# GNN kernel on one Trainium2 core: relational edges sorted by type, multiplied tile by tile, and gathered back in destination order

## The reference, cut to what matters

```python
x = _layernorm(x + sage3(x))          # per layer: mean of x[src] over dst, @ Wl + bl + x @ Wr
x = _layernorm(x + gin(x))            # gelu(x[src] + edge_attr @ bond_W) * edge_weight1, summed, MLP
x = _layernorm(x + gcn2(x))           # x[src] weighted and summed, layer norm, time embedding
x = _layernorm(x + rgcn2(x))

def _rel_conv(h, W, loop_w, b, src, dst, etype, relu):     # W: (8, 128, 128)
    h_rel = jnp.einsum('ni,rio->rno', h, W)
    msg = h_rel[etype, src]
    agg = jax.ops.segment_sum(msg, dst, num_segments=h.shape[0])
    out = agg + h @ loop_w + b
    return jax.nn.relu(out) if relu else out
```

## Time and profile before

| | us |
|---|---|
| three runs | 6101.26, 6092.66, 6088.61 |
| median | 6092.66 |
| profiled execution | 6085.37 |
| its span | 6083.6 |
| setup and round 0 (SAGE) | 0 to 624 |
| round 1, round 2 (SAGE) | 624 to 1120, 1120 to 1793 |
| round 3 (GIN) | 1793 to 2726 |
| rounds 4, 5 (GCN) | 2726 to 3439, 3439 to 4307 |
| rounds 6, 7 (RGCN) | 4307 to 5166, 5166 to 6084 |

### The profile page before, as it was taken

The page is one execution under the profiler, slowest core; times in us unless marked ns, Lnnn a source line. Parts: engine busy times, 40 slices in busy tenths (PEclk is TensorE's granted clock), DMA queues, the critical chain, the costliest instruction groups (busy, mean ns, idle before and its releaser), DMA issues.

```text
span 6083.6 us, 129573 instructions
## 1 busy us (share of the span) xinstructions
PE 4641.5 (76%) x25128; PEld 2978.4 (49%) x25129; DVE 3341.9 (55%) x10510; ACT 2416.6 (40%) x4967; POOL 1918.2 (32%) x1886
## 2 busy tenths in 40 slices
PE   5889678566668888866667477887688897788885
PEld 3555345233335555534444244554466674666662
DVE  4334233355644545545777477776454554676775
ACT  1333233144426777634555256564211111222233
POOL 5550663444213333006440233410323320423310
PEclk9999799788979999988889788898799999999998
DMA  3554466354424444324444255553333333333332
GB/s 101 171 173 143 143 206 217 99 159 158 148 82 128 144 142 137 127 93 127 143 143 132 76 178 189 185 182 123 109 108 120 113 112 125 96 111 113 104 106 97
DMA packets 443920, 815.61 MB, mean 134 GB/s; under 512 B 70873, under 2 KB 76819, under 8 KB 443829
## 3 DMA queue, kind: packets, MB, share of 16 engines
q1 hardware_dynamic: 389172, 697.28, 34.4%
q0 software_dynamic: 54656, 117.32, 7.7%
HBM read 480.10 MB, written 334.22 MB: 134 GB/s over the span
## 4 chain that ended last, share of the span: by engine, by line
PE 42%; issue 18%; DVE 15%; DVEq 8%; another core or an unknown queue 6%; ACT 4%; DMA 2%; POOL 2%; ACTq 2%; SPq 1%; POOLq 0%
PE p_agg L1115 7%; PE p_edge L1102 6%; PE p_agg L1117 6%; PE p_tr L1102 5%; PE p_agg L1148 4%; DVE onehot L1549 3%; DVE stats L1636 3%; PE p_wide L1235 2%; DVEq L371 2%; PE p_agg L1141 2%; PE p_dense L1191 2%; DVEq L1549 2%; PE p_wide L1179 2%; DVE u L1675 1%
## 5 line engine op out<-in xcount | busy, mean ns | idle before, releaser
L1115 PE MATMUL p_agg<-onehot,msg 128*128 128x512 f16 (+1 forms) x2848 | 1187.9, 417 | 793.4 <-DVE onehot L1549 490.6
L1549 DVE TENSOR_SCALAR onehot<-iota,dst_f,negbase 128x512 f16<-128x512 f16 (+1 forms) x2848 | 1040.3, 419 | 981.8 <-issue 382.7
L679 POOL DMA_INDIRECT raw<-node_s,src_i x980 | 960.8, 980 | 1843.1 <-DMA node_s<-o 695.6
L1117 PE MATMUL p_agg<-onehot,msg 128*128 128x512 f16 (+1 forms) x2848 | 1191.7, 418 | 25.8 <-issue 25.0
L1115 PEld LDWEIGHTS p_agg<-onehot,msg 128*128 x2848 | 290.2, 102 | 1171.1 <-issue 1035.3
L679 POOL DMA_INDIRECT raw<-node_x,src_i x392 | 378.6, 966 | 637.9 <-DMA feature<-more_masked 303.5
L1148 PE MATMUL p_agg<-h_in,w 128*128 128x512 f32 x784 | 470.6, 685 | 88.9 <-issue 46.1
L880 ACT ACTIVATE o<-v_ring,nmr,rstd 128x128 f32 (+1 forms) x1176 | 472.3, 482 | 59.0 <-DVE nmr L1652 47.3
L1636 DVE BATCH_NORM_STATS2 stats<-v_ring 128x6 f32 (+1 forms) x1960 | 418.2, 279 | 55.0 <-DVE v_ring L1626 19.0
L1117 PEld LDWEIGHTS p_agg<-onehot,msg 128*128 x2848 | 290.4, 102 | 280.6 <-issue 113.1
L1514 DVE SCALAR_TENSOR_TENSOR hid<-type_in,p_wide 128x512 f32<-128x512 f32 (+2 forms) x456 | 260.1, 617 | 289.8 <-PE p_edge L1102 190.6
(11 more groups left out here) (260 smaller groups left out, 7806.3 us busy)
## 6 DMA issues: line engine op xcount, KB each, us to landing
node_s<-o SPq DMA_DIRECT2D x392, 256.0 KB
h_in<-feature SPq DMA_DIRECT2D x392, 256.0 KB
feature<-u SPq DMA_DIRECT2D x294, 256.0 KB
node_x<-o SPq DMA_DIRECT2D x294, 256.0 KB
res_in<-node_x SPq DMA_DIRECT2D x294, 256.0 KB
h_in<-node_s SPq DMA_DIRECT2D x196, 256.0 KB
h_t<-dinv_scratch SPq DMA_DIRECT2D x196, 256.0 KB
h_in<-in_x SPq DMA_DIRECT2D x98, 256.0 KB
```

The source lines that it names most:

```text
L679: nc.gpsimd.indirect_dma_start(out=raw[:, (e % RING) * BATCH + j, :], out_offset=None, in_=src_d, in_offset=bass.IndirectOffsetOnAxis(ap=s ...
L1115: nc.tensor.matmul(p_agg[:, a, :], tile_ap(msg, t, 0, D), oh, start=first, stop=True, skip_group_check=True)
L1117: return nc.tensor.matmul(p_agg[:, a, :], tile_ap(msg, t, D, 2 * D), oh, start=False, stop=True, skip_group_check=True)
L1549: return V.tensor_scalar(tile_ap(onehot, slot), iota[:, :], dst_f[:, bass.ds(t, 1)], negbase[:, bass.ds(it * 2 + a, 1)], ALU.subtract, ALU ...
```

## The change

Between rounds 1 and 2 the edges of each batch are sorted by type on the chip. DVE and PE count, for each edge, the edges of its batch with a lower type or with the same type ahead of it; that gives its place in the sorted batch (`place_i`), the type of each place (`type_rows`, to DRAM), and for each batch a list of 14 *slots* in two words: which of the seven sorted tiles slot n works on. The type of slot n is n minus its tile, since sorted tiles hold types in steps. In round 2 POOL scatters the source numbers to their sorted places (196 scatters of 128 numbers), and they are read back as `sorted_i`.

In the relational rounds POOL gathers the rows in sorted order and copies them to `edge_fixed`. PE turns all seven tiles at once; DVE makes 14 masks of 128 columns instead of 16 of 512 or 384; PE makes 14 products instead of 56. Tile and type of a slot come from registers. ACT and DVE write the two fp16 parts to `stage`, ACT stores it to DRAM (`edge_dram`, 458 KB a batch), and POOL gathers the rows back into `msg` in destination order, seven more indirect DMAs a batch (`bring_back`). Batches run one ahead of before (`later_batches`). PE waits, before the items of each half, until the last batch that the half needs is back. In the text of the diff, `before` in names stands for earlier edges.

```diff
+SLOTS = BATCH + REL - 1
...
+            def scatter_sources(e):
+
+                if e == 0:
+                    pool.wait_ge(places_ready, 1)
+                for t in range(e * BATCH, (e + 1) * BATCH):
+                    nc.gpsimd.indirect_dma_start(
+                        out=sorted_dram, out_offset=bass.IndirectOffsetOnAxis(ap=place_i[:, t:t + 1], axis=0),
+                        in_=src_i[:, t:t + 1], in_offset=None).then_inc(scattered, 16)
+
+            def typed_edges(r, src_d):
+                q = S[r]
+
+                def gather(e):
+                    if e >= RING:
+                        wait(pool, q.batch_in, e - RING + 1)
+                    gather_batch(r, src_d, e, sorted_i)
+                    if e >= RING:
+                        wait(pool, q.masked_done, SLOTS * (e - RING + 1))
+                    pool.dma_start(type_in[:, e % RING, :], type_dram[e:e + 1, :].partition_broadcast(P)
+                                   ).then_inc(gathered[e % RING], 16)
+
+                def hand_over(e):
+                    slot = e % RING
+                    pool.wait_ge(gathered[slot], 16 * (per_batch[r] * (e // RING + 1) + landed_before[r]))
+                    if e:
+                        wait(pool, q.et_done, e)
+                    nc.gpsimd.tensor_copy(edge_fixed, raw[:, slot * BATCH:(slot + 1) * BATCH, :]
+                                          ).then_inc(q.batch_in.semaphore, 1)
+
+                def bring_back(e):
+                    wait(pool, q.staged, 16 * (e + 2))
+                    wait(pool, q.backed, 16 * BATCH * e)
+                    for t in range(e * BATCH, (e + 1) * BATCH):
+                        nc.gpsimd.indirect_dma_start(
+                            out=msg[:, t, :], out_offset=None, in_=edge_dram[0:(e + 1) * BATCH * P, :],
+                            in_offset=bass.IndirectOffsetOnAxis(ap=place_i[:, t:t + 1], axis=0),
+                        ).then_inc(q.backed.semaphore, 16)
+
+                pool.wait_ge(sorted_in, 16)
+                for e in range(2):
+                    gather(e)
+                    hand_over(e)
+                bring_back(0)
+                gather(2)
+                hand_over(2)
+                for e in range(1, BATCHES):
+                    if e + 2 < BATCHES:
+                        gather(e + 2)
+                    bring_back(e)
+                    if e + 2 < BATCHES:
+                        hand_over(e + 2)
...
                 for e in range(BATCHES):
...
                     gather_batch(r, src_d, e)
...
+                    if r == 2 and e >= RING:
+                        scatter_sources(e - RING)
...
                     if rel:
-                        for part, (j0, j1) in enumerate(QUARTERS):
-                            wait_apart(act, q.masked_used, e * (2 * REL) + (REL * (part + 2)))
-                            nc.scalar.activation(
-                                msg[:, bass.ds(e * BATCH + j0, j1 - j0), 0:D],
-                                related[part][:, 0:(j1 - j0) * D].rearrange("p (j d) -> p j d", d=D), ACT.Copy
-                                ).then_inc(q.hi_done.semaphore, 1)
+                        mine = bass.ds((e % 2) * BATCH, BATCH)
+                        wait_apart(act, q.masked_used, e + 2)
+                        nc.scalar.activation(stage[:, mine, 0:D],
+                                             related[:, 0:BATCH * D].rearrange("p (j d) -> p j d", d=D), ACT.Copy
+                                             ).then_inc(q.hi_done.semaphore, 1)
+                        wait_apart(act, q.lo_done, e + 1)
+                        wait_apart(act, q.staged, e * 16 + 16)
+                        nc.scalar.dma_start(
+                            edge_dram[bass.ds(e * (BATCH * P), BATCH * P), :].rearrange("(p j) d -> p j d", j=BATCH),
+                            stage[:, mine, :]).then_inc(q.staged.semaphore, 16)
...
-                def products(e, part):
-                    j0, j1 = QUARTERS[part]
-                    for m in range(REL):
-                        wait(pe, q.masked_done, e * (2 * REL) + (part * REL + m + 1))
-                        for j in range(j1 - j0):
-                            last = nc.tensor.matmul(
-                                related[part][:, j * D:(j + 1) * D], masked[m][:, j * P:(j + 1) * P],
-                                w[:, m, :], start=m == 0 and j == 0, stop=True, skip_group_check=True)
-                        last.then_inc(q.masked_used.semaphore, 1)
+                def products(e):
+
+                    these = slot_list(pe, PT, e)
+                    wait_apart(pe, q.lo_done, e)
+                    nc.tensor.matmul(related[:, 2 * HALF - 1:2 * HALF], ident[:, :], ident[:, 0:1], start=True, stop=True,
+                                     skip_group_check=True)
+                    for n in range(SLOTS):
+                        tile = slot_tile(pe, these, n)
+                        wait_apart(pe, q.masked_done, e * SLOTS + (n + 1))
+                        last = nc.tensor.matmul(
+                            related[:, bass.ds(tile * D, D)], masked[n],
+                            tile_ap(w, (n - tile).with_bounds(min_val=0, max_val=REL - 1)),
+                            start=n == 0, stop=True, skip_group_check=True)
+                    last.then_inc(q.masked_used.semaphore, 1)
...
                     t0, i0, i1 = these[:3]
+                    if rel:
+                        last_batch = pe.snap(((((t0 + (i1 - i0) * GROUP + (EVERY - 1)).with_bounds(
+                            min_val=0, max_val=TILES - 1) * ROW7) >> 16) & 31).with_bounds(
+                            min_val=0, max_val=BATCHES - 1))
+                        wait_apart(pe, q.backed, last_batch * (16 * BATCH) + 16 * BATCH)
...
-                        if rel:
-                            wait_apart(pe, q.lo_done, these[0] * 2)
...
-                def masks(e, part):
-                    j0, j1 = QUARTERS[part]
-                    wait_apart(dve, q.et_done, e * 2 + (part + 3))
-                    cols = slice(0, (j1 - j0) * P)
-                    for m in range(REL):
-                        wait(dve, q.masked_used, e * (2 * REL) + (part * REL + m + 1))
+                def masks(e):
+                    these = slot_list(dve, PT, e)
+                    wait_apart(dve, q.et_done, e + 1)
+                    wait_apart(dve, q.masked_used, e + 1)
+                    for n in range(SLOTS):
+                        tile = slot_tile(dve, these, n)
                         V.scalar_tensor_tensor(
-                            out=masked[m][:, cols],
-                            in0=flat(type_in[:, bass.ds(e % RING, 1), j0 * P:j1 * P]), scalar=float(m),
-                            in1=p_wide[:, part, cols], op0=ALU.is_equal, op1=ALU.mult
+                            out=masked[n],
+                            in0=types_flat[:, bass.ds((e % RING) * (BATCH * P) + tile * P, P)],
+                            scalar=colf[:, bass.ds((n - tile).with_bounds(min_val=0, max_val=REL - 1), 1)],
+                            in1=turned_batch[:, bass.ds(tile * P, P)], op0=ALU.is_equal, op1=ALU.mult
                             ).then_inc(q.masked_done.semaphore, 1)
...
                 if rd.kind == SAGE:
                     sage_round(r, rd.layer, False)
+                    if rd.layer == 1:
+                        sort_types()
```

297 lines of the change are left out of this document (210 added, 87 removed).

## The result

The changed kernel takes 7109.34 us (median of 4 runs, 7095.45 to 7134.94) against 6090.64 (median of 4, 6080.6 to 6101.26: the three of before and one more): a ratio of 1.1682, 95% interval 1.165 to 1.1713. Slower, as forecast, but by 1019 us where the forecast had 254, and beyond the range's upper end of 6640.

The account below looks back on a forecast made before the run. PE was taken to bound the first relational round, with DVE close behind in the second. Seven terms summed to +254 us on 6085.4, with 7.3 for the median 6346 us; range 5985 to 6640.

Parts of the forecast that it names:

- Term 3: First relational round: 14 register-addressed products instead of 56 shorten each batch's burst by 2.5 us, −70 us (−224 to +40).
- Term 7: Relational rounds: seven more indirect DMAs per batch fit POOL but slow the other engines, +129 us (0 to 314).
- term 2: Round 2: issuing 196 scatters of source numbers costs other engines 1.7 us per run of seven, +41 us (0 to 67).
- term 4: Second relational round: masks no longer made a batch ahead, so products come 2.0 us later per batch, +57 us (−116 to +90).
- Term 1: Between rounds 1 and 2: sorting in DVE's program ahead of round 2 costs +22 us (0 to 40).
- Terms 5 and 6: Computed tile numbers before each half's items, +50 us (0 to 67), and a lower granted PE clock, +25 us (0 to 50).
- term 5: PE before each half's items: the wait for returned rows is never late, but computing tile numbers costs +50 us (0 to 67).
- B: Rival: products were the bound and slots cost only the datapath's 0.28 us, 5835 us; chance 0.23 with half-way cases.
- C: Rival: slots are register-bound, but POOL's DMA issues cost the other engines nothing, 6176 us; chance 0.16.
- D: Rival: POOL's chain of staging, gathering back and hand-over becomes the bound, 6600 us (6480 to 6700); chance 0.14.

## Why the prediction was wrong

The sign was right, and so was the suspicion that POOL's issues cost others; the size was wrong by a factor of four. Term 3, the gain that the change was made for, had the wrong sign, so the right sign of the sum came from costs alone. PE's *turn* below is the time of PE from the end of a pair's row work, over products and transposes, to the next one-hot matmul, a mean over the batches of a round: before 14.7 and 14.2 us, without bring-back 16.9 and 22.4, changed 20.9 and 26.3, fixed slots without bring-back 8.3 and 13.5 (these kernels ran on different chips; 2% of a turn is 0.3 to 0.5 us).

**Term 7, and with it term 2, are where it failed.** "The other engines pay again what term 2 shows" took a run of seven as the unit of price. The rows it stood on the earlier trace rows were right, but a run of fourteen isn't two of seven. By the counted shares only the last four of a run's 8.8 us cost, and the second seven of one run cost all of theirs (10.1 us a batch for 8.8 us more of issuing). Term 7 was +129 (0 to 314); taking the bring-back out gives 384. Term 2 was +41 (0 to 67); taking the scatters out gives 226, since POOL there runs two batches' gathers and scatters, broken only by the weighings of 1.7 us, in stretches of some 38 us. The upper bounds, 5.6 us a run and 67 us, came from the same unit, so the range was too narrow as well. The row that would have told is of before: late register operations lie only in the second half of a run. I had counted how many there are, and not when.

**Terms 3 and 4 failed by as much: the slot's pace was right, the rest of the turn not.** Without bring-back the relational rounds lose 387 us, where terms 3 to 6 together had 62. A slot takes 0.78 us (forecast 0.72): fourteen take 11.0 us when POOL is quiet. But the transposes behind them take 1.70 us at a granted clock of 0.50 (the lower of its two levels) in place of 0.93 at full clock; the 0.6 of the prediction stands in no row that it names. And the longer instruction streams of a turn meet even the run of seven: in the first relational round fourteen products take 12.8 us in the mean. In the first relational round without bring-back the turn is 2.2 us longer than before, where I had it 2.5 shorter. In the second it is 8.2 longer (forecast 2.0), because DVE's first mask comes later than the 5.8 us I took: PE waits 7.7 us for it in the mean over that round. One of the longer waits, from the end of the row work to the first product:

```profile
5905.78 0.60 PE L1367 MATMUL p_dense<-ident,u 128*128 128x128 f32 x4
5906.06 0.69 ACT L956 ACTIVATE u<-p_agg,bias 128x512 f32<-128x512 f32 x1 [2.08 <-PE p_agg L1277]
5906.21 0.28 PE L1220 MATMUL p_pair<-ident 128*128 128x1 f32 x2
...
5909.29 0.64 DVE L1839 BATCH_NORM_AGGREGATE mv<-stats 128x2 f32<-128x6 f32 x8
...
5915.30 0.35 DVE L1715 SCALAR_TENSOR_TENSOR hid<-type_in,colf,p_wide 128x128 f32 x1 [5.37 <-issue]
...
5916.22 11.00 PE L1225 MATMUL p_pair<-w,hid 128*128 x28 [9.73 <-DVE hid L1715]
```

PE waits 9.7 us; DVE is done with its statistics at 5909.9 and needs 5.4 more until the first mask, for the loop's bounds and two list loads (0.74 and 0.90) at the end of POOL's run. With slots fixed this wait is still 5.7 in the mean, the 5.8 that the prediction named: half of the masks are no longer made a batch ahead. Term 3's real 2.2 and these 5.8 in full make 8.0 of the 8.2: term 4 failed by building on term 3's 2.5 us of gain and by letting PE catch up part of the wait.

**Term 1** was right where the sort is, and not at the end of the round: DVE's first low part of round 2 starts at 1157.09 against 1134.16, +22.9 for a forecast of +22. But without the scatters round 2 takes 663 us against 657, so most of the 22.9 is made up within it.

```profile
1157.09 1.08 DVE L1746 TENSOR_TENSOR msg<-raw,msg  x1
```

**Terms 5 and 6** together were +75. The rest of a batch's time outside the turn, without bring-back, is 17.5 and 19.0 us against 16.0 and 18.6: 1.5 x 28 + 0.4 x 28 = 53 us, not told apart. The premise of term 5, that rows are back long before their half, held: PE waited 17.1 and 3.8 us for them in all. The clock did fall, further than I said (to 0.67 and 0.64), while PE stood idle. What it cost alone wasn't measured: the transposes at the lower level are 0.77 us a batch, 43 us over the two rounds if all of it lies on the path, and keeping PE busy with further matmuls returned nothing net.

**The rivals.** B needed slots at the datapath's price (its sum has a slip of 6 us: 13.2 less 3.9 is 9.3, not 9.1); with slots fixed and no bring-back the turn is 6.4 us shorter than before in the first relational round, but the change as made has 0.78 a slot. C (POOL's issues cost nobody) is refuted by the seven more gathers and by every broken run. It is where the Trainium skill's page "Runtime: NRT & Kernel Launch", section "Instruction fetch mechanics", would have led, with instruction fetch in straight code hidden beneath dispatch. What follows from it, that straight code pays nothing for POOL's issues, the trace doesn't bear out: the masks of one batch, straight code, come 2.4 to 3.6 us apart. Whether it is the fetch that is late is not shown. D was nearest in size (6600) and wrong in mechanism: POOL's chain isn't late, it waits for the staged rows (18.6 and 25.4 us a batch in the mean of the two rounds), PE hardly waits for it, and more work on it made the kernel faster. At most the 111 + 32 us that are left once slots are fixed and runs are short could be its.

Added up where before takes 5951.5 us, of 1011 us: bring-back 384 (forecast 129), scatters 226 (41), and 401 for the rest (84 with terms 1 and 3 to 6), nearly all of it in the relational rounds; fixed slots return more than this rest (470).

## What to carry to other kernels

Count indirect DMAs of POOL not by number but by how long they run without a break: here five microseconds were nearly free, each further one was nearly lost to the other engines' issue, and a break of 0.85 us of other POOL work between them bought 3.8% of this kernel. The rewrite of its products, even with slots fixed and no bring-back, saved 108 us in the relational rounds and lost 250 in round 2. Idle time ended by "issue" on all engines at once, beside a busy POOL, is how it looks. A change that trades matmuls for register-addressed ones should be priced at the sequencer's pace (here 0.78 us for a matmul with two addresses from registers and a wait, against 0.22 with fixed addresses at full clock and 0.43 at half), and a product that other engines' steps are placed around has to keep what is made ahead.

## What the runs showed of the hardware

- While POOL issues indirect DMAs of 128 rows (0.94 us each, 1.25 apart) without a break, register operations of the other engines that take 0.04 to 0.1 us begin to take 0.7 after some 5 us, and plain weight loads come 1.4 to 2.1 us apart, which is two or three times 0.7. Seven direct DMAs of POOL behind such a run (3.8 us), or as many consecutive rows by ACT's queue, cost nothing measurable, and the slow issue is over within 1 us of the last indirect DMA there, and within 2 to 2.5 us of it behind runs of fourteen.
- The long operations of different engines keep step. In the second relational round of the changed kernel DVE has 202 of them, of which 43 end within 0.04 us of a long one of PE and 52 within 0.04 us of one of ACT; with DVE's times shifted by 0.35 us no end falls so close to one of PE's. So what is late looks common to the engines, and not each one's own.
- What in the issuing it is that holds up the others was not found out. The traces have two queues of instruction packets (8 or 16 KB each). In the relational rounds of the changed kernel they carry 33 packets in some 2540 us, and of 56 runs with three or more long operations 43 have none from 2 us ahead of the run to its end. So it isn't the packets of these two queues that come late; how else instructions reach an engine the traces don't show.
- A break of 0.83 to 0.85 us behind the fourth of seven is enough: in the relational rounds at most 9% of the others' operations are long in each of the four microseconds behind it. Yet in the changed kernel the copy of 0.93 us between seven and seven more didn't help: 49% of the operations in the three microseconds behind it are long (second relational round). It isn't that POOL goes on without a wait there: the weighing of 1.7 us in round 2 has DMAs behind it 0.17 us later as well, and in the three microseconds behind it at most 1% are long, or 3% when the kernel was run again. A shorter break worked behind four DMAs and a longer one behind fourteen, so how long it has to be may depend on the run ahead of it; no run here varied that alone.
- Two chips differ by 1.9% in the same kernel before (6066.8 and 5951.5 us).
